# A kernel of four transformer layers: work of the first feed-forward made within the first attention's tiles

## The chip, the core and the metric

The kernel runs on one core of a Trainium2 chip. Its engines work from queues of their own: TensorE (PE) for matmuls and transposes, VectorE (DVE), ScalarE (ACT), GpSimd (POOL) and SyncE (SP), which here only starts DMAs. Engines wait for one another through semaphores. The metric is the time of the whole program on the device, in microseconds.

## The reference

x has 8 samples of 256 positions and 256 channels, the context 77 positions a sample. The part that matters is the first layer:

```python
x = x + _L0_xattn_ref(ctx_1024, _layernorm(x), mask, ...)   # 16 heads of 16
x = x + _L0_ffn_ref(_layernorm(x), w1, conv_w, conv_b, w2)

def act_quant(x):
    scale = 127.0 / clip(max(abs(x), axis=-1), 1e-05)
    return clip(round(x * scale), -128, 127) / scale
def weight_quant(w):
    scale = 1.0 / clip(mean(abs(w)), 1e-05)
    return clip(round(w * scale), -1, 1) / scale
def bit_linear(x, w): return einsum('bsd,hd->bsh', act_quant(x), weight_quant(w))
h = bit_linear(x, w1)                  # 256 -> 1024
h = silu(depthwise_conv1d(h, conv_w, conv_b))    # 3 taps
return bit_linear(h, w2)               # 1024 -> 256
```

Three further layers follow (an attention with normed heads and a mixture of experts, an attention with a position bias and a routed spline, a feed-forward with the context as weights and a ternary linear layer). The change leaves them alone, but for the centring of two weights of the second attention.

## The kernel before

The program is written engine by engine. Each engine runs through the same stages, att0 (first attention), ffn0 (first feed-forward), att1 and eight more; behind each, stage_end makes the four computing engines wait for one another. Within a stage the order of an engine's work is written out by hand, and every instruction waits in that order.

**att0** works on 16 tiles of 128 positions (u = 0 to 15, two a sample). TensorE makes the scores of tile u+2 (L775) into four banks of PSUM; VectorE adds the mask (L402) and takes the largest of each head (L404); GpSimd subtracts it (L554); ScalarE takes the exponentials (L636); TensorE transposes them (L785), multiplies by the values (L802), VectorE divides by the sums (normed: L411, L412), TensorE transposes that (turned: L809) and projects it (L815), VectorE adds it to X (residual: L419). In its pass u of the loop TensorE does: transposes of tile u, turned(u-1), scores(u+2), the value products of tile u with projected(u-1) between, and then in most passes the transposes (L738, even u) or the query product (L757, odd u) of a sample to come. VectorE does: normed(u-1), scores(u+2), residual(u-1), at u = 5 centered(), and then the statistics of a sample to come (even u: L364 to L369) or its normalisation z (odd u: L377), until u = 9. GpSimd does: the subtraction of tile u+2, and in even passes the bias added to X (L541) and a reciprocal square root (L545).

centered() subtracts from two weights of the second attention their mean over each head (a sum L426, a factor L427 and a subtraction L428 each) and makes four small scales (L429 to L432).

**ffn0** begins behind stage_end with what nothing else covers. VectorE: the statistics of samples 0 and 1 (L912 to L917); the sums of absolute values of w1 and w2 (L988); TensorE adds these over the partitions (L1099); VectorE makes the means and scales (L991 to L993), the ternary w1 in three passes (L900 to L902), two memsets of the edges of f_G, the first quantised sample (quantized(0): L924 to L936), and then the three passes over w2. GpSimd clears the value blocks of the second attention (L520) and makes 8 diagonal taps of the convolution (L1042). TensorE then transposes the quantised sample (L1108, L1110), ScalarE copies that out, TensorE makes the hidden products in four pairs (L1121), VectorE scales each (hidden: L943), and the convolution is 48 matmuls a sample (L1131).

f_w1 and f_w2, the weights as loaded, have lain at the head of the buffer "big" since about 30 us. The quantised ones, f_G and the taps lie in the part of big that the attention's tiles use; the first sample's z, its statistics and the like lie in the buffer scr, which the tiles use too.

Of the kernel before, what the change touches and what calls it, by code (L numbers as in the profile page):

```python
# [113 lines left out]
def program(nc, pack0, pack1, pack2, x_in, ctx_in, ctxT_in, w1T_in, w2T_in, ew1_in, ew2_in, out):  # L114
    with ExitStack() as ctx:
# [240 lines left out]
        def att_dve(v, ch, lay):  # L356
# [24 lines left out]
            def scores(u):  # L381
# [15 lines left out]
                else:  # L397
                    add = a_mask[:, t, :].unsqueeze(1).unsqueeze(1).broadcast_to([P, 4, C, 2 * S2])
# [22 lines left out]
            def centered():  # L421

                v.wait_ge(in_ffn, 48)
                for name, wsum in zip(("wk1", "wq1"), a_wsum):
# [61 lines left out]
            for u in range(NT + 1):  # L486
# [11 lines left out]
                if lay == 0 and u == 5:  # L498
                    centered()
# [30 lines left out]
        def att_pool(g, lay):  # L530
# [43 lines left out]
            for u in range(NT):  # L574
# [127 lines left out]
        def att_pe(pe, lay):  # L702
# [58 lines left out]
            def scores(u):  # L761
# [105 lines left out]
        f_w1q = cut(C * FF, dt=BF16).rearrange("p (c n) -> p c n", c=C)  # L867
        f_w2q = cut(FC * D, dt=BF16).rearrange("p (c n) -> p c n", c=FC)
        f_G = cut(FC * (S + 2)).rearrange("p (f s) -> p f s", f=FC)
        f_taps = cut(FC * 3 * P).rearrange("p (f j n) -> p f j n", f=FC, j=3)  # L870
        cut = Cut(scr)
        f_y = [cut(FC * S).rearrange("p (f s) -> p f s", f=FC) for _ in range(2)]
        f_aq = cut(FC * S, dt=BF16).rearrange("p (f s) -> p f s", f=FC)
        f_z = cut(T * D).rearrange("p (t d) -> p t d", t=T)
        f_zq = cut(T * D, dt=BF16).rearrange("p (t d) -> p t d", t=T)
        f_zT = cut(C * S, dt=BF16).rearrange("p (c s) -> p c s", c=C)
        f_wide1 = cut(T * P).rearrange("p (t n) -> p t n", t=T)
# [5 lines left out]
        f_stats = [cut(T * 6).rearrange("p (t s) -> p t s", t=T) for _ in range(2)]  # L883
        f_mv = [cut(T * 2).rearrange("p (t s) -> p t s", t=T) for _ in range(2)]
        f_ve = [cut(T) for _ in range(2)]
        f_rstd = [cut(T) for _ in range(2)]
# [11 lines left out]
        def ternary(ch, v, src, dst, inv):  # L898

            ch.link(v.tensor_scalar(src, src, inv, ROUND, ALU.mult, ALU.add))  # L900
            ch.link(v.tensor_scalar(src, src, ROUND, 1.0, ALU.subtract, ALU.min))
            ch.link(v.tensor_scalar(dst, src, -1.0, None, ALU.max))  # L902
# [3 lines left out]
        def ffn0_dve(v, ch):  # L906
            s = ffn0

            def stats_of(i):
                b = i % 2  # L910
                for t in range(T):
                    ch.inc(v.bn_stats(f_stats[b][:, t, :], X[:, T * i + t, :]))  # L912
                ch.sync()
                for t in range(T):
                    ch.inc(v.bn_aggr(f_mv[b][:, t, :], f_stats[b][:, t, :]))
                ch.sync()
                v.tensor_scalar(f_ve[b], f_mv[b][:, :, 1], EPS, None, ALU.add).then_inc(var_ready, 1)  # L917

            def quantized(i):

                b = i % 2
                v.wait_ge(rstd_ready, i + 1)
                for t in range(T):
                    ch.inc(v.tensor_scalar(f_z[:, t, :], X[:, T * i + t, :], f_mv[b][:, t, 0:1], f_rstd[b][:, t:t + 1],  # L924
                                           ALU.subtract, ALU.mult))
                ch.sync()
                ch.link(v.tensor_reduce(f_am, f_z[:, :, :], AX.X, ALU.max, apply_absolute_value=True))
                ch.link(v.tensor_scalar(f_am, f_am, 1e-5, None, ALU.max))
                ch.inc(v.tensor_scalar(f_deq, f_am, f_mean127[:, 0:1], None, ALU.mult))
                ch.link(v.reciprocal(f_sc, f_am))  # L930
                ch.link(v.tensor_scalar(f_sc, f_sc, 127.0, None, ALU.mult))
                v.tensor_copy(f_wide1, f_deq.unsqueeze(2).broadcast_to([P, T, P])).then_inc(s["wide1_ready"], 1)
                for t in range(T):
                    ch.inc(v.tensor_scalar(f_z[:, t, :], f_z[:, t, :], f_sc[:, t:t + 1], ROUND, ALU.mult, ALU.add))
                ch.sync()
                v.tensor_scalar(f_zq, f_z[:, :, :], ROUND, None, ALU.subtract).then_inc(z_ready, T)  # L936
# [46 lines left out]

            stats_of(0)
            stats_of(1)
            v.wait_ge(in_ffn, 48)
            for n, (f_w, wq) in enumerate(((f_w1, f_w1q), (f_w2, f_w2q))):
                v.tensor_reduce(f_tot[:, n:n + 1], f_w, AX.X, ALU.add,  # L988
                                apply_absolute_value=True).then_inc(s["wsum_ready"], 1)
            v.wait_ge(s["wsum_psum"], 1)  # L990
            ch.link(v.tensor_scalar(f_mean, bank(0, 2), 1.0 / (FF * D), 1e-5, ALU.mult, ALU.max))  # L991
            ch.inc(v.tensor_scalar(f_mean127, f_mean, 1.0 / 127.0, None, ALU.mult))
            ch.link(v.reciprocal(f_inv, f_mean))  # L993
            ternary(ch, v, f_w1, f_w1q.rearrange("p c n -> p (c n)"), f_inv[:, 0:1])
            ch.inc(v.memset(f_G[:, :, 0:1], 0.0))
            v.memset(f_G[:, :, S + 1:S + 2], 0.0).then_inc(s["w_ready"], 1)
            quantized(0)
            ternary(ch, v, f_w2, f_w2q.rearrange("p c n -> p (c n)"), f_inv[:, 1:2])
            v.sem_inc(s["w_ready"], 1)
            hidden(0)  # L1000
            for i in range(B):
                if i + 1 < B:
                    quantized(i + 1)
                if i:
                    scales(i - 1)
                if i + 2 < B:
                    stats_of(i + 2)
# [12 lines left out]

        def ffn0_pool(g):
            s = ffn0

            def rstd_of(i):
                g.wait_ge(var_ready, i + 1)
                g.tensor_tensor(f_rstd[i % 2], f_ve[i % 2], neghalf[:, 0:T], ALU.pow).then_inc(rstd_ready, 1)
# [9 lines left out]
            rstd_of(0)  # L1036
            rstd_of(1)
            vb_zeroed(g, 1)
            g.wait_ge(in_ffn, 48)
            taps = w["conv_w"].rearrange("p (f j) -> p f j", j=3)  # L1040
            for f in range(FC):
                g.tensor_tensor(f_taps[:, f, :, :], ident.unsqueeze(1).broadcast_to([P, 3, P]),  # L1042
                                taps[:, f, :].unsqueeze(2).broadcast_to([P, 3, P]), ALU.mult).then_inc(s["taps_ready"], 1)
            for i in range(B):
                if i:
                    scaled(i - 1)
                if i + 2 < B:
                    rstd_of(i + 2)
# [47 lines left out]
        def ffn0_pe(pe):  # L1096
            s = ffn0
            pe.wait_ge(s["wsum_ready"], 2)
# [1721 lines left out]
```

## Time and profile before

| | us |
|---|---|
| median of 3 runs | 1440.86 (1433.71 to 1441.57) |
| the profiled execution | 1436.02, its span 1434.2 |
| PE busy / DVE / ACT / POOL, of the span | 1131.8 / 843.7 / 381.1 / 470.4 |
| mean granted clock of TensorE | 0.857 of full |
| first attention's tiles | about 33 to 160 |
| start of the first feed-forward until its convolution | about 160 to 184 |

The page of the profile has, for each engine, the busy time and the idle time with its releaser. A chain is read from the timeline: a start, a duration, and in brackets how long the engine had been idle and whose end released it. A large sum of busy time says nothing of one stage; the windows view gives it for a stretch.

### The profile page before, as it was taken

To read this page: it belongs to the slowest core of one execution; us is meant where nothing else is said; L and a number is where in the kernel's file an instruction comes from. 1 tells how busy PE (TensorE), PEld (TensorE's weight loads), DVE (VectorE), ACT (ScalarE), POOL (GpSimd) and SP (SyncE) were. 2 spreads that over 40 slices of the span, in tenths; PEclk is the share of its full clock that TensorE was granted. 3 is DMA by queue.
4 is the path that set the end of the run, shared out by engine and by line. 5 is a ranking of instruction groups with operands and counts; after the bars stand their busy time and mean duration, and the time that the engine had idled before them with its cause. 6 is when DMAs were issued, how large, how long until landed. Compare 5 with 4: busy or idle time off the path is not lost.

```text
span 1434.2 us, 20425 instructions
## 1 busy us (share of the span) xinstructions
PE 1131.8 (79%) x7256; PEld 947.5 (66%) x7256; DVE 843.7 (59%) x1935; ACT 381.1 (27%) x798; POOL 470.4 (33%) x340
## 2 busy tenths in 40 slices
PE   6889488885688968999849999999828997915765
PEld 4778376664477845888739999999727786603433
DVE  3776678765476645888722222222575776097895
ACT  2445132221355511111112222222303443201111
POOL 3533412244556211568571100040423332002220
PEclk9799799998699989899969999999956997556575
DMA  7999000000000020000154321121200000000000
GB/s 288 392 387 363 1 0 1 19 1 0 1 1 1 2 83 1 1 1 30 55 224 152 131 84 71 37 82 46 66 24 0 1 1 1 0 0 1 15 23 22
DMA packets 43731, 93.57 MB, mean 65 GB/s; under 512 B 3821, under 2 KB 17806, under 8 KB 40838
## 3 DMA queue, kind: packets, MB, share of 16 engines
q1 hardware_dynamic: 35254, 62.24, 12.0%
q0 software_dynamic: 7104, 29.14, 5.6%
q10 hardware_dynamic: 1296, 1.18, 0.2%
q8 instruction: 47, 0.77, 0.2%
q14 instruction: 30, 0.25, 0.1%
HBM read 39.02 MB, written 51.51 MB: 63 GB/s over the span
## 4 chain that ended last, share of the span: by engine, by line
PE 65%; DVE 20%; issue 5%; ACT 4%; POOL 3%; DMA 1%; POOLq 0%; DVEq 0%; SPq 0%; ACTq 0%
PE PS L1857 9%; PE PS L1867 9%; PE PS L802 7%; PE PS L1740 3%; PE PS L1131 3%; PE PS L815 3%; PE PS L785 3%; PE PS L1394 3%; PE PS L775 3%; PE PS L757 2%; PE PS L1729 2%; PE PS L2567 2%; PE PS L684 2%; PE PS L754 1%; PE PS L1766 1%
## 5 line engine op out<-in xcount | busy, mean ns | idle before, releaser
L1857 PEld LDWEIGHTS PS<-scr 128*128 128x128 f32 x992 | 118.1, 194 | 5.1 <-issue 1.8
L1857 PE MATMUL PS<-scr 128*128 128x128 f32 x992 | 120.1, 279 | 1.5 <-ACT scr L1885 1.4
L554 POOL TENSOR_TENSOR scr<-scr,big 128x1232 f32<-128x1232 f32 x32 | 72.0, 2249 | 147.8 <-DVE big L404 147.8
L1867 PE MATMUL PS<-scr 128*128 128x256 f32 x496 | 112.2, 379 | 0.0
L1890 ACT ACTIVATE scr<-PS,W 128x128 f32<-128x128 f32 x148 | 53.5, 367 | 192.6 <-PE PS L1857 192.6
L1920 DVE TENSOR_SCALAR scr<-PS,W 128x128 f32<-128x128 f32 x148 | 51.3, 350 | 85.4 <-PE PS L1857 85.4
L641 ACT ACTIVATE big<-PS 128x512 f32<-128x512 f32 x144 | 74.6, 525 | 96.4 <-PE PS L785 96.3
L1867 PEld LDWEIGHTS PS<-scr 128*128 128x128 f32 x496 | 91.8, 190 | 11.2
L785 PE MATMUL PS<-W,scr 128*128 128x128 f32 x480 | 82.3, 294 | 21.1 <-ACT scr L636 8.1
L802 PEld LDWEIGHTS PS<-scr,big 128*128 128x128 f32 x640 | 85.2, 200 | 7.2 <-issue 5.5
L1926 DVE TENSOR_TENSOR scr<-PS,W 128x256 f32<-128x256 f32 x37 | 15.7, 425 | 124.9 <-PE PS L1867 124.9
L802 PE MATMUL PS<-scr,big 128*128 128x34 f32 (+1 forms) x640 | 87.4, 279 | 0.0
L1131 PE MATMUL PS<-big 128*128 128x256 f32 x384 | 85.5, 379 | 0.0
L785 PEld LDWEIGHTS PS<-W,scr 128*128 128x128 f32 x480 | 60.7, 158 | 32.5 <-issue 8.8
L1131 PEld LDWEIGHTS PS<-big 128*128 128x128 f32 x384 | 71.7, 190 | 9.6
L1033 POOL TENSOR_TENSOR scr<-scr 128x1024 f32<-128x1024 f32 x16 | 37.3, 2352 | 106.2 <-ACT scr L1061 106.2
L1964 POOL DMA_DIRECT2D expert_out<-scr x28 | 15.2, 544 | 163.5 <-DVE scr L1926 161.1
L1740 PE MATMUL PS<-W,scr 128*128 128x128 f32 x512 | 64.8, 288 | 2.0 <-DVE scr L1499 2.0
L1740 PEld LDWEIGHTS PS<-W,scr 128*128 128x128 f32 x512 | 62.6, 203 | 2.8 <-issue 2.7
L636 ACT ACTIVATE scr<-scr 128x1232 f32<-128x1232 f32 x48 | 58.7, 1223 | 13.7 <-POOL scr L554 12.2
L549 POOL TENSOR_TENSOR big<-big,neghalf 128x32 f32<-128x32 f32 x8 | 43.5, 5434 | 47.4 <-DVE big L437 47.4
L815 PE MATMUL PS<-W,big 128*128 128x256 f32 x192 | 54.5, 407 | 1.4 <-ACT big L646 1.4
(393 smaller groups left out, 2448.7 us busy)
## 6 DMA issues: line engine op xcount, KB each, us to landing
expert_in<-zeros SPq DMA_DIRECT2D x1, 19712.0 KB, 60.5
expert_out<-zeros SPq DMA_DIRECT2D x1, 19712.0 KB, 111.8
scr<-ew_in POOLq DMA_DIRECT2D x12, 1024.0 KB, 6.3
scr<-expert_in SPq DMA_DIRECT2D x38, 128.0 KB, 2.0
big<-ew_in POOLq DMA_DIRECT2D x4, 1024.0 KB, 8.3
expert_out<-scr POOLq DMA_DIRECT2D x28, 128.0 KB, 2.0
W<-pack SPq DMA_DIRECT2D x1, 2458.0 KB, 10.0
W<-pack SPq DMA_DIRECT2D x1, 2152.0 KB, 8.6
```

Of the source, the lines that this page charges most:

```text
L554: g.tensor_tensor(sc3, sc3, a_mx[u % 3].unsqueeze(2).broadcast_to([P, H, S2]), ALU.subtract).then_inc(s["sub_ready"], 1)
L636: a.activation(a_sc[lay][u % 3], a_sc[lay][u % 3], ACT.Exp, scale=scale).then_inc(s["p_ready"], 1)
L641: a.activation(a_PT[u % 2][:, 4 * g:4 * g + n, :], bank(ring_bank(lay, "p", u, g), n * P).rearrange("p (c n) -> p c n", c=n), ACT.Copy).th ...
L785: ins = pe.transpose(bank(b, P, k * P), a_sc[lay][u % 3][:, at:at + P], ident)
L802: ins = pe.matmul(bank(6 + u % 2, n * (DH + 1), FIRST[c] * (DH + 1)), a_PT[u % 2][:, c, :], a_VB[lay][:, c, 0:n, u // T, :], start=(c == 0 ...
L815: ins = pe.matmul(bank(6 + u % 2, D, D), a_OT[:, c, :], wo[:, c, :], start=(c == 0), stop=(c == C - 1))
L1131: ins = pe.matmul(bank(2 + p % 2, S, (f % 2) * S), f_taps[:, f, j, :], f_G[:, f, j:j + S], start=(j == 0), stop=(j == 2))
L1740: ins = pe.matmul(bank(4, P, c * P), vp[:, t, c * P:(c + 1) * P], ident, start=(t == 0), stop=(t == B - 1))
L1857: ins = pe.matmul(bank(1 + f % 4, G), e_w1[slot][:, k, f * P:(f + 1) * P], e_xT[:, k, :], start=(k == 0), stop=(k == C - 1))
L1867: ins = pe.matmul(bank(5 + t, D), e_h[:, f, t * P:(t + 1) * P], e_w2[slot][:, f, :], start=(f == 0), stop=(f == FC - 1))
L1890: a.activation(e_h[:, f, :], bank(1 + f % 4, G), ACT.Relu, bias=moe_bias(e, f)).then_inc(s["h_act"], 1)
L1920: v.tensor_scalar(e_h[:, f, :], bank(1 + f % 4, G), moe_bias(e, f), 0.0, ALU.add, ALU.max).then_inc(s["h_dve"], 1)
```

## The change

The work that prepares the first feed-forward moves into the passes of att0. VectorE, between residual(u-1) and the statistics or z of its pass: at u = 1 and 2 the sums of w1 and w2; before the scores of tile 6 (pass 4) the means, and behind residual in that pass the scales; at u = 5 to 10 one pass over a weight each; at u = 11 to 13 centered(), now in three parts, which leaves u = 5; at u = 14 and 15 the statistics of samples 0 and 1, and at u = 15 quantized(0). TensorE's cross-partition sum comes before the scores of tile 6, into two unused columns of bank 0. GpSimd makes two taps each at u = 11 to 14, and the two reciprocal square roots behind its loop. ffn0 keeps the two memsets and begins with the transposes. So that all this can lie there, f_w1q gets memory of its own, f_w2q and the taps take the place of the weights as loaded, and z and its statistics move to a free part of big. The core of the diff:

```diff
@@ att_dve, scores(u) @@
+                    if lay == 0 and u == MEANS_AT:
+                        weight_means_dve(v, ch)
@@ att_dve, the loop, behind residual(u - 1) @@
-                if lay == 0 and u == 5:
-                    centered()
+                if lay == 0:
+                    if u in (1, 2):
+                        weights_dve(v, ch, u - 1)
+                    if u == MEANS_AT - 2:
+                        weight_scales_dve(v, ch)
+                    if 5 <= u <= 10:
+                        weights_dve(v, ch, u - 3)
+                    if 11 <= u <= 13:
+                        centered(u - 11)
+                    if u in (14, 15):
+                        v.wait_ge(s["y_done"], PTILE(0, 2 * (u - 14) + T))
+                        ternary_stats(v, ch, u - 14)
+                    if u == 15:
+                        quantized(v, ch, 0)
@@ att_pool, the loop @@
+                if lay == 0 and 11 <= u <= 14:
+                    taps_pool(g, 2 * (u - 11))
+                    taps_pool(g, 2 * (u - 11) + 1)
...
+            if lay == 0:
+                ternary_rstd(g, 0)
+                ternary_rstd(g, 1)
@@ att_pe, scores(u) @@
+                if lay == 0 and u == MEANS_AT:
+                    pe.wait_ge(ffn0["wsum_ready"], 2)
+                    pe.matmul(bank(0, 2, 510), ones, f_tot, start=True, stop=True).then_inc(ffn0["wsum_psum"], 1)
@@ new @@
+        def weights_dve(v, ch, part):
+
+            s = ffn0
+            if part < 2:
+                if part == 0:
+                    v.wait_ge(in_ffn, 48)
+                v.tensor_reduce(f_tot[:, part:part + 1], (f_w1, f_w2)[part], AX.X, ALU.add,
+                                apply_absolute_value=True).then_inc(s["wsum_ready"], 1)
+                return
+            n, step = divmod(part - 2, 3)
+            src, inv = (f_w1, f_w2)[n], f_inv[:, n:n + 1]
+            if step == 0:
+                ch.link(v.tensor_scalar(src, src, inv, ROUND, ALU.mult, ALU.add))
+            elif step == 1:
+                ch.link(v.tensor_scalar(src, src, ROUND, 1.0, ALU.subtract, ALU.min))
+            else:
+                ch.link(v.tensor_scalar((f_w1q, f_w2q)[n].rearrange("p c n -> p (c n)"), src, -1.0, None, ALU.max))
+                v.sem_inc(s["w_ready"], 1)
+        MEANS_AT = 6
@@ ffn0_dve @@
-            stats_of(0)
-            stats_of(1)
-            v.wait_ge(in_ffn, 48)
...
-            v.wait_ge(s["wsum_psum"], 1)
...
-            ternary(ch, v, f_w1, f_w1q.rearrange("p c n -> p (c n)"), f_inv[:, 0:1])
             ch.inc(v.memset(f_G[:, :, 0:1], 0.0))
             v.memset(f_G[:, :, S + 1:S + 2], 0.0).then_inc(s["w_ready"], 1)
-            quantized(0)
-            ternary(ch, v, f_w2, f_w2q.rearrange("p c n -> p (c n)"), f_inv[:, 1:2])
-            v.sem_inc(s["w_ready"], 1)
             hidden(0)
@@ ffn0_pool @@
-            rstd_of(0)
-            rstd_of(1)
             vb_zeroed(g, 1)
-            g.wait_ge(in_ffn, 48)
...
-            for f in range(FC):
...
@@ ffn0_pe @@
-            pe.wait_ge(s["w_ready"], 1)
             normed(0)
             for p in range(PAIRS):
                 hidden(0, p)
             pe.wait_ge(s["taps_ready"], FC)
+            pe.wait_ge(s["w_ready"], 3)
```

## Rows read from the trace of the kernel before

**Rows 1.** Windows: stretch, length, busy us of PE PEld DVE ACT POOL, PEclk, DMA.
```profile
33.00:160.00 127.00, 110.18 (x888) 95.94 (x888) 85.02 (x128) 55.31 (x98) 49.14 (x29) 0.91 0.88 332
...
160.00:182.00 22.00, 3.44 (x16) 2.27 (x16) 20.34 (x35) 2.15 (x3) 14.18 (x11) 0.51 0.00 0
```

**Rows 2.** Timeline, 160 to 185 us: start, duration, engine, line, what; source view of L1042.
```profile
162.19 4.47 DVE L988 TENSOR_REDUCE small<-big 128x1 f32<-128x2048 f32 x2
...
163.00 3.51 POOL L520 MEMSET scr<- 128x4080 f32 x1
...
168.21 1.74 DVE L900 TENSOR_SCALAR big<-big,small 128x2048 f32<-128x2048 f32 x1
...
177.91 1.28 DVE L900 TENSOR_SCALAR big<-big,small 128x2048 f32<-128x2048 f32 x1
...
178.09 0.45 PE L1108 MATMUL PS<-W,scr 128*128 128x128 f32 x1 [10.73 <-DVE scr L936]
...
180.20 1.89 PE L1121 MATMUL PS<-scr,big 128*128 128x256 bf16 x8 [1.02 <-ACT scr L1068]
...
181.94 1.29 DVE L943 TENSOR_TENSOR big<-PS,scr 128x512 f32<-128x512 f32 x2 [0.23 <-DVE big L902]
...
184.37 10.55 PE L1131 MATMUL PS<-big 128*128 128x256 f32 x48
...
L1042 POOL TENSOR_TENSOR big<-W x8: 835/870/1819, 166.5 to 175.0; 128x384 f32<-128x384 f32 x8
```

**Rows 3.** VectorE's timeline: first statistics, and one quantisation alone.
```profile
159.91 0.75 DVE L912 BATCH_NORM_STATS2 scr<-X 128x6 f32<-128x256 f32 x2
...
185.20 0.73 DVE L924 TENSOR_SCALAR scr<-X,scr 128x256 f32<-128x256 f32 x2
...
188.34 0.43 DVE L936 TENSOR_SCALAR scr<-scr 128x512 bf16<-128x512 f32 x1
```
**Rows 4.** Timeline, end of an odd turn (1).
```profile
55.00 2.25 POOL L554 TENSOR_TENSOR scr<-scr,big 128x1232 f32<-128x1232 f32 x1 [4.56 <-DVE big L404]
...
55.40 2.32 DVE L377 TENSOR_SCALAR scr<-X,big 128x256 f32<-128x256 f32 x2
...
58.54 0.38 PE L809 MATMUL PS<-W,big 128*128 128x128 f32 x2
```

**Rows 5.** Timeline, end of an even turn (2).
```profile
62.72 2.25 POOL L554 TENSOR_TENSOR scr<-scr,big 128x1232 f32<-128x1232 f32 x1 [5.47 <-DVE big L404]
...
64.19 0.80 DVE L369 TENSOR_SCALAR big<-big 128x2 f32<-128x2 f32 x1
...
64.92 1.26 POOL L541 TENSOR_TENSOR X<-X,W 128x512 f32<-128x512 f32 x1
...
65.67 0.44 PE L809 MATMUL PS<-W,big 128*128 128x128 f32 x2 [0.81 <-DVE big L412]
```

**Rows 6.** Timeline, end of turn 5, with centered().
```profile
85.93 1.17 DVE L427 TENSOR_SCALAR small<-small 128x32 f32<-128x32 f32 x1
...
87.13 0.69 DVE L428 TENSOR_TENSOR W<-W,small 128x512 f32<-128x512 f32 x1
...
91.07 0.44 PE L809 MATMUL PS<-W,big 128*128 128x128 f32 x2 [2.54 <-DVE big L412]
```

**Rows 7.** Windows, 92 to 93 us; TensorE's timeline at the next turn.
```profile
92.00:93.00 1.00, 1.00 (x12) 0.84 (x7) 0.69 (x1) 0.00 (x0) 0.00 (x0) 0.62 1.03 387
...
100.56 0.38 PE L809 MATMUL PS<-W,big 128*128 128x128 f32 x2
```

**Rows 8.** Timelines of GpSimd and TensorE, ends of turns 10 and 12.
```profile
127.37 2.25 POOL L554 TENSOR_TENSOR scr<-scr,big 128x1232 f32<-128x1232 f32 x1 [5.48 <-DVE big L404]
...
129.35 0.38 PE L809 MATMUL PS<-W,big 128*128 128x128 f32 x2
...
141.26 2.25 POOL L554 TENSOR_TENSOR scr<-scr,big 128x1232 f32<-128x1232 f32 x1 [5.49 <-DVE big L404]
...
142.43 0.44 PE L809 MATMUL PS<-W,big 128*128 128x128 f32 x2
```

More of the change, by code:

```diff
@@ L419, in residual, with centered @@
                 v.tensor_tensor(X[:, u, :], bank(6 + u % 2, D, D), X[:, u, :], ALU.add).then_inc(s["y_done"], 1)
-            def centered():
-                v.wait_ge(in_ffn, 48)
-                for name, wsum in zip(("wk1", "wq1"), a_wsum):
+            def centered(part):
+                if part < 2:
+                    name, wsum = ("wk1", "wq1")[part], a_wsum[part]
                     w3 = w[name].rearrange("p (g d) -> p g d", d=DH)
@@ L882, in program @@
         f_amax = cut(S)
[L883 to L886, printed above, removed]
         f_am = csmall(T)
@@ L896, in program, with ternary_stats @@
                     "wide2_ready", "row2_psum", "row2_ready", "scaled_ready", "aq_ready", "o_psum", "o_kept")
[L898 to L902, printed above, removed]
+        def ternary_stats(v, ch, i):
+            b = i % 2
+            for t in range(T):
+                ch.inc(v.bn_stats(f_stats[b][:, t, :], X[:, T * i + t, :]))
+            ch.sync()
+            for t in range(T):
+                ch.inc(v.bn_aggr(f_mv[b][:, t, :], f_stats[b][:, t, :]))
+            ch.sync()
+            v.tensor_scalar(f_ve[b], f_mv[b][:, :, 1], EPS, None, ALU.add).then_inc(var_ready, 1)
@@ new lines, in quantized @@
+        def quantized(v, ch, i):
+            b = i % 2
+            v.wait_ge(rstd_ready, i + 1)
+            for t in range(T):
+                ch.inc(v.tensor_scalar(f_z[:, t, :], X[:, T * i + t, :], f_mv[b][:, t, 0:1], f_rstd[b][:, t:t + 1],
+                                       ALU.subtract, ALU.mult))
+            ch.sync()
+            ch.link(v.tensor_reduce(f_am, f_z[:, :, :], AX.X, ALU.max, apply_absolute_value=True))
+            ch.link(v.tensor_scalar(f_am, f_am, 1e-5, None, ALU.max))
+            ch.inc(v.tensor_scalar(f_deq, f_am, f_mean127[:, 0:1], None, ALU.mult))
+            ch.link(v.reciprocal(f_sc, f_am))
+            ch.link(v.tensor_scalar(f_sc, f_sc, 127.0, None, ALU.mult))
+            v.tensor_copy(f_wide1, f_deq.unsqueeze(2).broadcast_to([P, T, P])).then_inc(ffn0["wide1_ready"], 1)
+            for t in range(T):
+                ch.inc(v.tensor_scalar(f_z[:, t, :], f_z[:, t, :], f_sc[:, t:t + 1], ROUND, ALU.mult, ALU.add))
+            ch.sync()
+            v.tensor_scalar(f_zq, f_z[:, :, :], ROUND, None, ALU.subtract).then_inc(z_ready, T)
@@ new lines, in weight_means_dve, with weight_scales_dve, taps_pool @@
+        def weight_means_dve(v, ch):
+            v.wait_ge(ffn0["wsum_psum"], 1)
+            ch.link(v.tensor_scalar(f_mean, bank(0, 2, 510), 1.0 / (FF * D), 1e-5, ALU.mult, ALU.max))
+        def weight_scales_dve(v, ch):
+            ch.inc(v.tensor_scalar(f_mean127, f_mean, 1.0 / 127.0, None, ALU.mult))
+            ch.link(v.reciprocal(f_inv, f_mean))
+        def taps_pool(g, f):
+            if f == 0:
+                g.wait_ge(ffn0["w_ready"], 2)
+            taps = w["conv_w"].rearrange("p (f j) -> p f j", j=3)
+            g.tensor_tensor(f_taps[:, f, :, :], ident.unsqueeze(1).broadcast_to([P, 3, P]),
+                            taps[:, f, :].unsqueeze(2).broadcast_to([P, 3, P]), ALU.mult).then_inc(ffn0["taps_ready"], 1)
@@ L907, in ffn0_dve @@
             s = ffn0
[L909 to L936, printed above, removed]
             def hidden(i):
@@ L1002, in ffn0_dve @@
                 if i + 1 < B:
-                    quantized(i + 1)
+                    quantized(v, ch, i + 1)
                 if i:
@@ L1097, in ffn0_pe @@
             s = ffn0
-            pe.wait_ge(s["wsum_ready"], 2)
-            pe.matmul(bank(0, 2), ones, f_tot, start=True, stop=True).then_inc(s["wsum_psum"], 1)
             def normed(i):
```

40 lines of the change are left out of this document (18 added, 22 removed).

## The prediction, made before the changed kernel was run

> **What bounds the kernel now.** I read the trace in the order in which the change meets it. First the busy time by stretch [rows 1]: in the first attention's tiles (33 to 160 us) TensorE is busy 110 of 127 us, VectorE 85; in the 22 us behind them TensorE is busy 3.4 us and VectorE 20.3 us. So there are two regimes, and the change takes work out of the second and puts it into the first.
>
> Then the handover [rows 2]. VectorE's first instruction of the feed-forward is at 159.91 [rows 3]. From there two sums of absolute values (2.28 us each), one cross-partition sum on TensorE, the means, three passes over w1 and the first quantisation run one behind the other, until TensorE gets its first transposes at 178.09; the convolution begins at 184.37. Nothing on TensorE covers this: 24.5 us from 159.91 to 184.37 is a pure chain.
>
> Then one tile of the attention, as a chain of turns. I call turn u what the engines do in pass u of the loops, and mark its start by TensorE's transposes L809 (turned(u-1)). VectorE's order in a turn is normed(u-1), scores(u+2), residual(u-1), the extras that the change adds to, statistics (even u) or z (odd u), and next normed(u), for which L809 of the next turn waits. The reader is to see two things in [rows 4, 5]. GpSimd starts L554 (2.25 us) just before VectorE's residual and is still in it when the extras begin. And a tensor_scalar of VectorE that meets it doesn't end before L554 does: in the odd turn two L377 take 2.32 us and end 0.47 behind L554's end (57.72 against 57.25), where such a pair alone takes 0.73 (L924, [rows 3]); in the even turn L369, two elements a partition, takes 0.80 and ends at 64.99, L554 at 64.97. In the turn with centered(), L427 ends at 87.10 in the same way after 1.17 us for 32 elements [rows 6]. So the free time that VectorE seems to have in a tile lies mostly elsewhere (it waits for the scores), and where the extras stand there is none: in odd turns L809 comes 3.54 us behind L554's start with z done 0.8 us before it, in even turns it comes 2.95 behind it, set by VectorE.
>
> **The change, part by part.**
>
> *Removed behind the tiles.* After the stage's end TensorE can transpose at once, since weights and z exist. What is left is the piece from 178.09 to 184.37, 6.3 us, less about 0.75: the first half of the eight L1121 was done near 181.15, L943 came at 181.94, behind the second weight's passes [rows 2]: 5.5 us. At full clock this piece would be about 1 us shorter; GpSimd's memset L520 of 3.5 us, which now starts together with this piece, may hold VectorE's two small memsets and so L943 by up to 1.3 us. So 24.5 - 5.5 = **19.0 us gained** (17.7 to 20.1). The second weight's passes ran beside other work and give no more. From the convolution on nothing differs.
>
> *Added to the tiles.* A weight pass takes 1.28 us with GpSimd idle and 1.74 us beside the taps [rows 2]; started behind a wait for L554 I take 1.2, since the start is then already paid (L377 above). The statistics of one sample took 1.15 (two of them from 159.91 to 162.19, [rows 2, 3]); as L369's end is late I count 1.2. From L554's start to L809 it gives: odd turns 2.25 + 1.2 + 0.73 (z) + 0.68 (normed and hand-over, the 64.99 to 65.67 of [rows 5]) = 4.86 against 3.54, **+1.32**; even turns 2.25 + 1.2 + 1.2 (statistics, which no longer run under L554) + 0.68 = 5.33 against 2.95, **+2.38**. Turn by turn:
> - Turns 1 and 2 have the sums of 2.28 us, which ran at this length beside GpSimd's memset and first tap [rows 2]. The extras begin 0.4 behind L554's start (55.40, [rows 4]). Turn 1: 0.4 + 2.28 + 0.73 + 0.68 = 4.1 against 3.54: +0.6. Turn 2: 0.4 + 2.28 + 1.2 + 0.68 = 4.6 against 2.95: +1.6.
> - Turn 4: the cross-partition sum on TensorE before the scores (two small matmuls, 0.3 to 0.6 us, 0.4 taken), the mean behind it fits into VectorE's wait for the scores; the scales are tensor_scalar and reciprocal, 0.4 us behind L554, with the statistics behind them: 4.53 against 2.95. Together +2.0.
> - Turn 5: centered() leaves (TensorE waited 2.54 us for it [rows 6]), a pass comes: 1.32 - 2.54 = -1.2. Turn 6: 7.13 + 2.38 = 9.5 us, against 9.5 before (91.07 to 100.56), when the clock was low [rows 7]: 0.
> - Turns 7 and 9 +1.3 each, turn 8 +2.4. Turn 10, without statistics: 4.13 against the 1.98 from 127.37 to 129.35 (L554, L809) [rows 8]: +2.15.
> - Turns 11 and 12: centered() in two parts. Each is a sum (beside L554), L427 (waits for L554) and L428 (0.69, [rows 6]). From L554's start 2.25 + 0.2 + 0.69 + 0.68 = 3.8, against 3.54 in turn 11, an odd one, and 1.17 in turn 12 [rows 8]: +0.3 and +2.6. L428 reads two tensors of SBUF, and behind L554 GpSimd now goes on with a tap (median 0.87 us, [rows 2]) or with L541 (1.26, [rows 5]). No row shows such an instruction of VectorE beside one of GpSimd; held, it costs 0.75 and 1.3 more. I take half: +0.6 and +3.3.
> - Turn 13: four tiny tensor_scalars behind L554, 3.1 against 1.2 as in turn 12, a tap may come between: +2.2. Turn 14: the first statistics, 1.2 us, ahead of normed(14): +1.2.
> - Turn 15: second statistics 1.2 and the first quantisation, 3.57 us from 185.20 to 188.77 [rows 3], both ahead of normed(15), which until now follows residual(14) with nothing between and has TensorE waiting for it. So all of it is on the path: 4.8, with the rstd on GpSimd between up to 5.3: +5.0.
>
> The sum is 0.6 + 1.6 + 2.0 - 1.2 + 0 + 1.3 + 2.4 + 1.3 + 2.15 + 0.6 + 3.3 + 2.2 + 1.2 + 5.0 = **22.5 us lost** (20 to 26). The rule of the Trainium skill that bears on it is in "SBUF — State Buffer", section "SBUF: two separate sides": the port pair that VectorE shares with GpSimd is an exclusive lock, kept for the whole instruction, for VectorE's two-port modes and for two SBUF inputs against a GpSimd instruction that reads SBUF. For the tensor_scalars the trace agrees (2.32 us for 0.73). For L428 no row here shows it; by the page turns 11 and 12 cost the whole 2.05 us, and the sum would be 23.5 instead of 22.5.
>
> The eight taps cost GpSimd 0.87 us each; in turns 11 to 13 it waits before L554 for 2 us or more ([rows 8] have 5.5 before those of turns 10 and 12), so two a turn fit, and their wait for the weights is met a turn earlier. Behind that wait would stand the next L554, due later. Nothing of SP's or of GpSimd's DMA queue moves. The new place of the buffers costs nothing.
>
> *The clock.* The wait of 2.54 us of turn 5 had a price of its own: the granted clock went from full (2.4 GHz) to half (1.2 GHz) at about 92.4, and the turn took 9.5 instead of 7.1 us [rows 7]: 2.4 us. In a plain even turn TensorE waits 0.81 us [rows 5]. Now it waits 2.5 us or more in turns 2, 4, 6, 8, 12, 13 and 15 and 2.1 in turn 10. Where a fall comes on an odd turn, the turn is bound by TensorE: 7.8 + 3.3 = 11.1, against 9.1, so about 2 us each (3 in turn 3). I can't tell how many of these waits drop the clock; none costs 0, nearly all cost 12. I take three, **6 us lost**.
>
> Net: 22.5 + 6 - 19.0 = **+9.5 us**. The profiled execution had 1436.0 us (span 1434.2, and 1.8 around it); the median of the runs is 1440.9, so it was one of the quicker. From one I get 1445.5, from the other 1450.4; I forecast **1448 us**.
>
> **The rivals.**
> 1. *The clock falls in nearly every second turn.* For it: the new waits are as long as the one that did it or longer. Against it: one fall is all that the trace has inside these tiles after their start, and one case says nothing of how often a wait of this length does it. Price 12 instead of 6: 1454. In the Trainium skill, "TensorE: Matmul & The Clock Gate", section "HAM oscillation — how this bites in real kernels", a loop that waits once in each pass goes back to half clock every pass; by it this rival would be the forecast. The trace has one such wait, and it agrees.
> 2. *Faster: VectorE's passes run beside L554.* If the large passes get through (they did get their turns between the taps, 1.74 us against 1.28), a pass costs 1.25 us right behind residual: odd turns hide it, even ones cost 0.7, turns 12, 13, 14 and 15 cost 1.7, 0.5, 1.2 and 4.8, turns 5 and 6 give back 2.7 and 1.7. Some 7.5 us lost against 19 won: -11.5, 1427. It decides at the point where the tiles grow by less than 19 us. Against it: every tensor_scalar that met L554 ended behind it.
> 3. *A draw.* The lock holds but costs less than I add up (15 to 18 us, few falls of the clock): -3 to +4, about 1438.
>
> **How the numbers follow.** Forecast 0.50 (its own range 1441 to 1455), rival 1 0.17, rival 2 0.12, rival 3 0.21. The range 1432 to 1461 leaves out rival 2 and the far end of rival 1. About 0.5% (7 us) is what a measurement can tell from no change. Slower by more: all of rival 1 and four fifths of the forecast, 0.57. Within: the rest of the forecast and nearly all of rival 3, 0.30. Faster: rival 2 and a little, 0.13.
>
> **What would show it.** In the changed kernel the weight passes (1.2 us of work) must read 2.5 to 3 us in the tiles and end about 1.2 behind L554; turn 8 must take 9.5, turn 15 9.7 us; the last residual comes 23 to 32 us later, the convolution begins 5.5 us behind the stage's end. I am wrong if passes of 1.25 us stand beside a running L554, if TensorE's waits before L809 stay under 1 us in turns 6 to 10, or if the stage after begins later than 7 us behind the tiles.

## The result, and the profile after

The changed kernel is slower: 1459.22 us (median of 4 runs, 1448.65 to 1463.21) against 1438.96 beside it, a ratio of 1.0153 with a 95% interval of 1.0113 to 1.0193. That is 20 us; the forecast was 1448, or 9.5 us more than before. The time lies in the stated range (1432 to 1461) and on the forecast side, but only 2 us under the top of that range and above the forecast's own (1441 to 1455): the loss is about twice what was summed.

The profiled execution of the changed kernel had 1463.2 us (span 1461.5), at the upper end of its runs. Its lines have other numbers: L554 is now L569, L541 is L556, L809 is L833, L815 is L839, L1121 is L1156, L1131 is L1166.

Windows view of the changed kernel, columns as in [rows 1]:

```profile
33.00:202.00 169.00, 134.10 (x885) 115.36 (x885) 103.02 (x158) 55.52 (x97) 60.39 (x39) 0.76 0.66 250
202.00:211.50 9.50, 7.36 (x28) 4.29 (x29) 2.46 (x6) 2.54 (x4) 3.50 (x1) 0.50 0.00 0
```

The stretch of the tiles has grown by over 40 us and the one behind it has shrunk from 22 to under 10. And there is one number that was 0.91 before: the granted clock of the tiles is 0.76 of full.

The handover, TensorE's timeline of the changed kernel (start, duration):

```profile
203.13 2.07 PE L839 MATMUL PS<-W,big 128*128 128x256 f32 x4 [0.47 <-ACT big L667]
205.84 0.47 PE L1143 MATMUL PS<-W,big 128*128 128x128 f32 x1 [0.64 <-DVEq L185]
...
211.55 11.69 PE L1166 MATMUL PS<-big 128*128 128x256 f32 x48
```

The transposes follow the last projection by 0.6 us, and the convolution begins 5.7 us behind their start. That is the piece of the old chain that is left, and it is as long as forecast (5.5 us). But the convolution begins at 211.55, where it began at 184.37 [rows 2]: 27.2 us later, the whole difference of the two spans (27.3). Behind it these two executions take 1249.8 and 1250.0 us. In the later experiments, on four chips, this rest took 1241 to 1262 us, within about 4 us of one another on one chip; so each kernel is compared only with runs of the kernel before beside it on its own chip.

An even turn (6), timelines of VectorE, GpSimd and TensorE of the changed kernel; compare [rows 5]:

```profile
107.29 2.25 POOL L569 TENSOR_TENSOR scr<-scr,big 128x1232 f32<-128x1232 f32 x1 [8.81 <-DVE big L406]
...
107.71 2.92 DVE L967 TENSOR_SCALAR big<-big 128x2048 f32<-128x2048 f32 x1
...
109.50 2.25 POOL L556 TENSOR_TENSOR X<-X,W 128x512 f32<-128x512 f32 x1
...
112.58 0.69 PE L833 MATMUL PS<-W,big 128*128 128x128 f32 x2 [3.15 <-DVE big L414]
```

The pass over the weights starts 0.4 us behind L569's start, takes 2.92 instead of 1.28 us and ends at 110.63, 1.1 behind L569's end (109.54). It then held off L556 in its turn, which took 2.25 instead of 1.26. TensorE waited 3.15 us. Now the clock, windows view at both ends of the fall that follows:

```profile
111.00:112.00 1.00, 0.00 (x0) 0.00 (x0) 0.93 (x6) 0.00 (x0) 0.77 (x2) 0.74 1.02 385
112.00:113.00 1.00, 0.42 (x2) 0.29 (x2) 0.49 (x2) 0.00 (x0) 0.68 (x1) 0.50 1.04 391
...
121.00:122.00 1.00, 1.00 (x4) 0.86 (x4) 1.00 (x1) 0.00 (x0) 0.00 (x0) 0.64 1.03 387
```

It is at half (1.2 GHz) from 111.5 to 121.7 us, nearly the whole of turn 7. In that turn VectorE's pass costs nothing:

```profile
117.67 2.25 POOL L569 TENSOR_TENSOR scr<-scr,big 128x1232 f32<-128x1232 f32 x1 [4.99 <-DVE big L406]
...
120.80 1.22 DVE L969 TENSOR_SCALAR f_w1q<-big 128x2048 bf16<-128x2048 f32 x1
...
124.67 0.38 PE L833 MATMUL PS<-W,big 128*128 128x128 f32 x2
```

TensorE is so late with L839 that the residual and the pass come after L569, the pass runs at its own 1.22 us, and TensorE doesn't wait at L833. This turn is bound by TensorE at half clock: 12.1 us.

All turns in us, from the starts of L809 or its successor. The forecast column has the 22.5 us of the port and the queue, without the 6 us of the clock. The last column is an experiment that is told below:

| turn | before | forecast | changed kernel (TensorE's wait at its end) | waits filled |
|---|---|---|---|---|
| 1 | 8.1 | 8.7 | 12.7 (0) | 12.7 |
| 2 | 7.1 | 8.7 | 8.7 (2.4) | 8.7 |
| 3 | 7.8 | 7.8 | 12.6 (0) | 7.8 |
| 4 | 7.1 | 9.1 | 8.8 (2.4) | 8.8 |
| 5 | 10.5 | 9.3 | 11.1 (0) | 9.0 |
| 6 | 9.5 | 9.5 | 9.5 (3.2) | 9.5 |
| 7 | 7.7 | 9.1 | 12.1 (0) | 12.0 |
| 8 | 7.1 | 9.5 | 9.5 (3.2) | 9.5 |
| 9 | 7.8 | 9.1 | 12.5 (0) | 9.0 |
| 10 | 6.2 | 8.3 | 8.5 (2.2) | 8.6 |
| 11 | 7.7 | 8.3 | 12.7 (0) | 8.5 |
| 12 | 5.3 | 8.6 | 8.9 (3.5) | 8.9 |
| 13 | 5.4 | 7.6 | 10.5 (0.4) | 8.1 |
| 14 | 4.7 | 5.9 | 5.6 (1.1) | 6.9 |
| 15 | 4.7 | 9.7 | 9.1 (5.5) | 9.1 |
| sum | 106.7 | 129.2 | 152.7 | 137.1 |

The even turns are as forecast to 0.3 us. The odd ones from 3 to 13 are 2 to 5 us longer than forecast. The clock fell behind each even turn up to 12 and behind turn 15, seven times. What I had taken as three falls at 2 us was six falls inside the tiles at some 3 us, one at their end, and one in turn 1, which the kernel before didn't have in its profiled execution.

The profiled executions are single draws: 46 us more in the tiles, 17.6 less behind them and a start 1.2 earlier give 27 us, where the medians differ by 20. An execution of 1448.65 us was among the runs of the changed kernel, with a granted clock of 0.858 over the whole where the profiled one had 0.848; its trace isn't there.

### The profile page after: what moved, and what is told of

It reads as the page before. It is cut to its first block, busy times and chain, and to the rows that moved or that the text cites. A ratio compares the mean times of both kernels' runs of the same rounds, so it can differ in the third digit from the quotient of the medians.

```text
span 1461.5 us, 20426 instructions
## 1 busy us (share of the span) xinstructions
PE 1157.0 (79%) x7256; PEld 966.9 (66%) x7256; DVE 842.2 (58%) x1935; ACT 381.3 (26%) x798; POOL 471.4 (32%) x340
## 4 chain that ended last, share of the span: by engine, by line
PE 65%; DVE 20%; issue 5%; ACT 4%; POOL 4%; DMA 1%; POOLq 0%; SPq 0%; DVEq 0%; ACTq 0%
PE PS L1890 9%; PE PS L1900 9%; PE PS L826 7%; PE PS L839 3%; PE PS L1166 3%; PE PS L1773 3%; PE PS L1427 3%; PE PS L778 3%; PE PS L809 3%; PE PS L799 3%; PE PS L1762 2%; PE PS L2600 2%; PE PS L705 1%; PE PS L833 1%; PE PS L775 1%
## 5 line engine op out<-in xcount | busy, mean ns | idle before, releaser
L569 POOL TENSOR_TENSOR scr<-scr,big 128x1232 f32<-128x1232 f32 x32 | 71.9, 2248 | 175.8 <-DVE big L406 175.8
L826 PEld LDWEIGHTS PS<-scr,big 128*128 128x128 f32 x640 | 95.1, 220 | 8.4 <-issue 5.9
L809 PE MATMUL PS<-W,scr 128*128 128x128 f32 x480 | 83.7, 297 | 20.9 <-ACT scr L657 8.1
L826 PE MATMUL PS<-scr,big 128*128 128x34 f32 (+1 forms) x640 | 96.3, 297 | 0.0
L1166 PE MATMUL PS<-big 128*128 128x256 f32 x384 | 86.6, 382 | 0.0
L809 PEld LDWEIGHTS PS<-W,scr 128*128 128x128 f32 x480 | 62.0, 161 | 32.8 <-issue 9.2
L1166 PEld LDWEIGHTS PS<-big 128*128 128x128 f32 x384 | 72.5, 192 | 9.9
L839 PE MATMUL PS<-W,big 128*128 128x256 f32 x192 | 61.1, 447 | 1.4 <-ACT big L667 1.4
L657 ACT ACTIVATE scr<-scr 128x1232 f32<-128x1232 f32 x48 | 58.7, 1223 | 13.5 <-POOL scr L569 12.0
```

The costliest lines, as they stand in the source:

```text
L569: g.tensor_tensor(sc3, sc3, a_mx[u % 3].unsqueeze(2).broadcast_to([P, H, S2]), ALU.subtract).then_inc(s["sub_ready"], 1)
L657: a.activation(a_sc[lay][u % 3], a_sc[lay][u % 3], ACT.Exp, scale=scale).then_inc(s["p_ready"], 1)
L809: ins = pe.transpose(bank(b, P, k * P), a_sc[lay][u % 3][:, at:at + P], ident)
L826: ins = pe.matmul(bank(6 + u % 2, n * (DH + 1), FIRST[c] * (DH + 1)), a_PT[u % 2][:, c, :], a_VB[lay][:, c, 0:n, u // T, :], start=(c == 0 ...
L839: ins = pe.matmul(bank(6 + u % 2, D, D), a_OT[:, c, :], wo[:, c, :], start=(c == 0), stop=(c == C - 1))
L1166: ins = pe.matmul(bank(2 + p % 2, S, (f % 2) * S), f_taps[:, f, j, :], f_G[:, f, j:j + S], start=(j == 0), stop=(j == 2))
```

## The experiments

**Port, queue or clock.** Three kernels put one more instruction of VectorE into the kernel before, in turns 6, 8 and 10, where the change puts its passes. One is a pass of tensor_scalar, one a sum of about the same length (an estimate from L404, 1.44 us for 1232 elements), one a sum of 2.28 us. A tensor_reduce didn't wait for GpSimd in the trace of before: L426 took 0.68 us both beside L554 and behind it. In these kernels L554 is L557, L541 is L544 and L809 is L812.

```diff
@@ kernel before, att_dve, behind residual(u - 1) @@
+                if lay == 0 and u in (6, 8, 10):
+                    v.wait_ge(in_ffn, 48)
+                    ch.link(v.tensor_scalar(f_w1, f_w1, 1.0, None, ALU.mult))
+                    ch.link(v.tensor_reduce(spare, f_w1[:, 0:1152], AX.X, ALU.add))
+                    ch.link(v.tensor_reduce(spare, f_w1[:, 0:2048], AX.X, ALU.add))
```

Each kernel has one of the last three lines: b_scalar_even the pass, b_reduce_same the sum over 1152 elements, b_reduce_long the one over 2048. The pass multiplies f_w1 by one in place, the sums are used by nothing.

> The kernel before, with one pass of tensor_scalar over w1 (128x2048, times 1.0) added behind the residual in turns 6, 8 and 10. Shared port and clock (my theory): the pass ends 1.2 us behind L554, turn 8 takes 9.5 instead of 7.2 us and turn 10 8.3 instead of 6.15, TensorE waits about 3.2 us before L809 and its clock falls behind each, so that turns 9 and 11 take about 12 instead of 7.7: in all 15 to 20 us slower. Port without clock: turns 9 and 11 stay at 7.7, 7 us slower. No port: turn 8 takes 7.9, in all 2 us slower.

> The kernel before, with a tensor_reduce of 1152 columns (about 1.3 us, as long as a pass of tensor_scalar alone) in the same three places; its result is used for nothing. My theory: it runs beside L554, so turn 8 takes 7.8 (plus 0.6), turn 10 6.5, TensorE waits 1.4 us, no fall of the clock, turns 9 and 11 stay at 7.7: 2 us slower in all. If the added work costs by its place in the queue and not by the port, it costs what the tensor_scalar costs.

> The kernel before, with a tensor_reduce of 2048 columns (2.28 us) in the same three places; its result is used for nothing. No port is held, but TensorE waits some 2.4 us before L809. If the wait alone drops the clock: turn 8 takes 8.8, turn 10 7.5 and turns 9 and 11 about 12: 4.6 us from the waits and 8 to 13 from the clock. If the clock theory is wrong: 4.6 us slower and turns 9 and 11 stay at 7.7.

Measured against the kernel before: 1.0103 (1.0048 to 1.0157), 1.0036 (1.0011 to 1.0062) and 1.0102 (1.0050 to 1.0154). The intervals overlap a little; it is the traces that tell the first two apart. Turn 8 in VectorE's and TensorE's timelines, first b_scalar_even:

```profile
119.53 2.92 DVE L502 TENSOR_SCALAR big<-big 128x2048 f32<-128x2048 f32 x1
...
124.40 0.69 PE L812 MATMUL PS<-W,big 128*128 128x128 f32 x2 [3.15 <-DVE big L412]
```

b_reduce_same:

```profile
114.46 1.34 DVE L502 TENSOR_REDUCE small<-big 128x1 f32<-128x1152 f32 x1
...
116.90 0.64 DVE L369 TENSOR_SCALAR big<-big 128x2 f32<-128x2 f32 x1
...
118.21 0.44 PE L812 MATMUL PS<-W,big 128*128 128x128 f32 x2 [2.03 <-DVE big L412]
```

b_reduce_long:

```profile
114.97 2.27 DVE L502 TENSOR_REDUCE small<-big 128x1 f32<-128x2048 f32 x1
...
119.20 0.69 PE L812 MATMUL PS<-W,big 128*128 128x128 f32 x2 [2.50 <-DVE big L412]
...
131.74 0.38 PE L812 MATMUL PS<-W,big 128*128 128x128 f32 x2
```

Two instructions of about 1.3 us that both start 0.4 us behind L557's start: the tensor_scalar takes 2.92, the tensor_reduce 1.34. Turn 8 takes 9.5 and 8.3 us, turn 10 8.3 and 6.7. So the port is real and worth 1.1 to 1.6 us a turn. My 7.8 for b_reduce_same was too low: its L369 now met the bias (L544, 116.25 to 117.51) and ended with it, 0.64 us for two elements. With that TensorE waited 2.03 us instead of the 1.4 expected, and its clock fell, which I had not expected either: 5 us slower, not 2.

The third kernel separates the clock. Its sum takes 2.27 us beside L557, as long as alone, so it doesn't meet the port, and yet after its wait of 2.50 us the next turn (9) takes 12.5 us. Turn 11, after a wait of 1.35, takes 7.8. After b_reduce_same's 2.03 turn 9 takes 11.1, after b_scalar_even's 3.15 it takes 13.5; before, it takes 7.8. Turns 9 and 11 have no added work in any of the three. They grow behind a long wait of TensorE, whether a port or a longer sum made it. In b_scalar_even two more turns grew: the fall behind turn 5 lasted 20 us, from 92.4 to 112.9, through turns 6 (10.7) and 7 (13.0).

**Filling the waits.** If that is so, the changed kernel must get its odd turns back when TensorE is kept busy with nothing, while VectorE's delays stay.

```diff
@@ changed kernel, att_pe, turned(u) @@
+                fill = {2: 8, 4: 8, 5: 4, 6: 8, 7: 4, 8: 8, 9: 4, 10: 8, 12: 8, 14: 4, 15: 20}.get(u, 0) if lay == 0 else 0
+                if fill:
+                    pe.wait_ge(s["y_done"], PTILE(lay, u))
+                    for _ in range(fill):
+                        pe.matmul(bank(6 + (u + 1) % 2, 128), ident, ident, start=True, stop=True)
                 pe.wait_ge(s["on_ready"], PTILE(lay, u) + 1)
```

This is a_filled_all. A first form, a_filled, had eight matmuls for u = 2, 4, 6, 8, 10 and 12 alone.

> The changed kernel, with eight matmuls of the identity by itself (about 1.8 us) issued by TensorE just before it waits for VectorE at the start of turns 3, 5, 7, 9, 11 and 13, into a bank that is free then; their result is used for nothing. Clock theory: the waits of 2.2 to 3.5 us shrink to 0.4 to 1.7, the clock stays at full, the odd turns 3 to 13 take 8 to 9 us instead of 11 to 12.7, the even ones stay as they are: 15 to 20 us quicker than the changed kernel. If the odd turns are long for another reason (the port, VectorE's work), nothing is won.

Measured 1.0097 (1.0076 to 1.0117): less than expected, 2 to 8 us quicker than the changed kernel by its 1.0112 and 1.0153 on other chips. Turns 3, 5, 7, 9, 11 and 13 took 7.8, 9.0, 9.2, 9.0, 8.4 and 8.9 us in the profiled execution, 52.3 in all instead of 71.5. But the clock now fell in turns 6 and 10, behind waits of 1.1 us at the end of odd turns, which had become bound by VectorE, in turn 13 behind one of 1.68, and still at the end. That is why the next form fills more. In this trace the convolution begins at 194.45, 17 us earlier than in the changed kernel; behind it this execution took 7.8 us more (1257.8).

The changed kernel itself (after_again) and the new form ran on one chip:

> The changed kernel once more, to stand beside the next two on one chip and to show how much the tiles differ from execution to execution. Theory: each wait of TensorE of 2 us or more is followed by a fall of the clock; the even turns take the same time to 0.1 us as in the first execution (8.7, 8.8, 9.5, 9.5, 8.5, 8.9), the odd ones differ with the moment of the fall.

> The changed kernel, with matmuls of no use ahead of every longer wait of TensorE in the tiles: eight in turns 3, 5, 7, 9, 11 and 13, four in turns 6, 8, 10 and 15, twenty in turn 16. If the long turns are the port plus the clock, as I say: the clock stays at full in the tiles, what is left is the port's part that the prediction summed, 22.5 us over the kernel before (turns 1 to 16 about 129 us, against 107), and it is 12 to 20 us quicker than the changed kernel on the same chip. If the clock isn't the cause, the turns stay as long as in the changed kernel.

On one chip: the changed kernel 1453.43 us, 1.0112 (1.0060 to 1.0164) of before; with its waits filled 1436.78 us, 1.0016 (0.9984 to 1.0048). The two intervals don't meet. So 14 us (by the ratios) to 17 us (by the medians) of the changed kernel's time are the clock's, and with the clock up it is as quick as the kernel before: the port's part and the handover's gain cancel. Two lines of windows of a_filled_all, first the tiles (from 49 to 202 us the changed kernel has 0.77), then the fall of turn 1 that is left in them:

```profile
49.00:187.00 138.00, 123.06 (x980) 109.07 (x980) 98.90 (x144) 50.58 (x90) 52.37 (x35) 0.93 0.69 262
51.00:60.00 9.00, 9.00 (x33) 8.03 (x33) 6.05 (x8) 1.50 (x2) 2.25 (x1) 0.50 1.05 410
```

The last column of the table has its turns. Against my expectation the clock didn't stay at full: falls are left in turn 1, in turn 7, behind a wait of 1.36 us, and in turn 14, from 172.7 to 176.2 us, behind one of 2.62 us at the end of turn 13, which had no fill. With 8.4 us for turn 1 (from a_filled), 9.0 for turn 7 (as turns 5 and 9) and 5.6 for turn 14 (as in the changed kernel, at full clock) its tiles would take 128.5, 22 us over before; 22.5 were forecast for the port and the queue.

after_again also shows how steady the pattern is: its sum of turns is 152.7 us again, and no turn differs by more than 0.1, the odd ones included, which I had expected to differ.

**The place.** The same six passes, put ahead of the scores:

```diff
@@ changed kernel, att_dve @@
+                if lay == 0 and 5 <= u <= 10:
+                    weights_dve(v, ch, u - 3)
                 if u + 2 < NT:
                     scores(u + 2)
...
-                    if 5 <= u <= 10:
-                        weights_dve(v, ch, u - 3)
```

> The changed kernel with the six weight passes of turns 5 to 10 put ahead of the scores, where VectorE waits for TensorE, instead of behind the residual. My theory: in even turns GpSimd is idle there and the pass costs nothing (turns 6 and 8 take 7.2, turn 10 6.2, no fall of the clock behind them), in odd turns it meets L556 and costs up to 1.3: turns 5 to 10 take about 47 us instead of 63, the whole is 14 to 18 us quicker than the changed kernel. If the amount of work decides and not its place: no gain.

Measured 1.0050 (1.0025 to 1.0075) against before. From turn 5 to the end of turn 10 it takes 49.4 us, the changed kernel 63.1. Turns 6, 8 and 10 take 7.2, 7.2 and 6.2 us, with no fall behind them. The 49.4 us still hold the fall behind turn 4, which makes turn 5 12.5 us. The changed kernel didn't run on this chip; by its ratios on two others (1.0153 and 1.0112) the new place is worth 9 to 15 us, where 14 to 18 were expected.

**The last turns.** The statistics and the quantisation, which the change puts behind the residual of turns 14 and 15, ahead of the scores of their turn (there are none in these turns) and so of the residual:

```diff
@@ changed kernel, att_dve @@
+                if lay == 0:
+                    if u in (14, 15):
+                        v.wait_ge(s["y_done"], PTILE(0, 2 * (u - 14) + T))
+                        ternary_stats(v, ch, u - 14)
+                    if u == 15:
+                        quantized(v, ch, 0)
                 if u + 2 < NT:
                     scores(u + 2)
```

The same lines behind the residual are gone.

> The changed kernel, with the first statistics and the first quantisation in turns 14 and 15 put ahead of the residual, where VectorE waits 3.4 us for TensorE, instead of behind it. My theory: turn 14 goes from 5.6 to 4.7, turn 15 from 9.1 to about 5.7 (statistics and quantisation are 4.8 us and the gap is 3.6), TensorE no longer waits 5.5 us, and the convolution begins 4 to 6 us earlier. If the place doesn't matter: no gain.

Measured 1.0118 (1.0082 to 1.0154), not to be told from the changed kernel by its time. The trace shows turns 14 and 15 with 4.5 and 5.6 us instead of 5.6 and 9.1, as expected, and a wait of 1.75 instead of 5.47 us at their end; this is 4.7 us of 1460. The clock ahead of it differed too: this trace has no fall in turns 1 and 11.

**Everything in the gaps.** The last two findings together:

```diff
@@ changed kernel, att_dve, between normed(u - 1) and scores(u + 2) @@
+                if lay == 0:
+                    for part in {0: (0,), 1: (1,), 4: (2,), 6: (3,), 8: (4,), 10: (5,), 12: (6, 7)}.get(u, ()):
+                        weights_dve(v, ch, part)
+                    if u in (11, 12):
+                        v.wait_ge(s["y_done"], PTILE(0, 2 * (u - 11) + T))
+                        ternary_stats(v, ch, u - 11)
+                    if u == 14:
+                        for part in range(3):
+                            centered(part)
+                    if u == 15:
+                        quantized(v, ch, 0)
```

In place of the block behind the residual. MEANS_AT is 4 with the scales right behind the means, and GpSimd makes four taps in pass 11 and two each in 12 and 14, the reciprocal roots in 12.

> All the moved work, each piece put where VectorE waits for TensorE and GpSimd is mostly idle: the sums ahead of the scores in turns 0 and 1, the passes ahead of the scores in turns 4, 6, 8, 10 and (two) 12, statistics in 11 and 12, centering in 14, quantisation in 15, both ahead of the residual. My theory: no turn grows by more than 1 us, no wait of TensorE is above 1.2 us, the clock stays at full from the first turns on, the tiles take about as long as before (110 us or less from turn 1 to the last), and the 19 us of the handover remain: 15 to 22 us quicker than the kernel before, 1.0 to 1.5%. If moved work always costs in the tiles what it saves behind them: no change against the kernel before.

Measured 1427.28 us, 0.9858 (0.9836 to 0.9879) of before: 20 us quicker than before. Turn 6 of it, VectorE:

```profile
92.47 1.22 DVE L965 TENSOR_SCALAR big<-big 128x2048 f32<-128x2048 f32 x1
94.00 1.44 DVE L405 TENSOR_TENSOR scr<-PS,big 128x1232 f32<-128x1232 f32 x1 [0.32 <-DVE big L965]
```

The pass stands in the gap of 1.3 to 1.5 us in which VectorE used to wait for the scores, GpSimd is idle, and the turn takes 7.2 us. The tiles take 109.7 us. Longer than before are turn 2 (7.7, the means), 12 (6.6), 14 (6.5) and 15 (5.4), in all 4.5 us, and turn 3: its clock fell, behind a wait of 1.27 us, and it took 11.1. So turns 3, 12 and 14 grew by more than the 1 us expected, and three waits (1.27, 1.23 and 1.80 us) were above 1.2. On the other side the fall of turn 6 is gone, since centered() has left turn 5. The convolution begins at 170.10, 14.3 us earlier than in the trace of before, which was taken with the first result and not beside this one; what makes up the other 6 us of the 20 no trace here shows.

Then it ran once more, unchanged (gaps_again), beside a kernel that also fills the waits that are left in it (gaps_warm):

```diff
@@ gaps, att_pe, turned(u) @@
+                fill = {2: 4, 12: 4, 14: 7, 15: 3}.get(u, 0) if lay == 0 else 0
+                if fill:
+                    pe.wait_ge(s["y_done"], PTILE(lay, u))
+                    for _ in range(fill):
+                        pe.matmul(bank(6 + (u + 1) % 2, 128), ident, ident, start=True, stop=True)
@@ gaps, ffn0_pe @@
+            for _ in range(6):
+                pe.matmul(bank(7, 128), ident, ident, start=True, stop=True)
```

> The kernel with all moved work in VectorE's gaps once more, beside the next one on the same chip: 1.2 to 1.6% quicker than the kernel before, as in its first run.

> The kernel with all moved work in VectorE's gaps, and matmuls of no use on TensorE ahead of its waits in turns 3 (four), 13 (four), 15 (seven) and 16 (three) and, six, behind the first transposes of the feed-forward. Clock theory: no fall in turn 3 (minus 3.3 us) and a full clock at the handover (from the last L831 to the convolution 7 us instead of 9.6): 3 to 6 us quicker than without them, 1.6 to 1.9% quicker than the kernel before. If the clock plays no part there: no gain.

The first measured 0.9877 (0.9826 to 0.9928), the second 0.9846 (0.9816 to 0.9876). In the trace of the second turn 3 took 7.8 us and the clock stayed at full from turn 2 through the handover. But turn 1 took 12.7 us at half clock in this execution. And gaps_again had no fall at the handover without any filling: its wait of 1.79 us at the end of turn 14 wasn't followed by one, where the 1.80 us of the first run were. From the last L831 to the convolution it took 6.9 us, the first run 9.6. So the convolution began at 167.11 us in gaps_warm and at 167.03 in gaps_again. The intervals overlap widely: a gain of the filling beyond the placing isn't shown.

## Why the prediction was right, and which term was too small

The way, slower, was right and rested on the right mechanisms. That the time also fell into the range is partly luck: two of the four runs (1461.7 and 1463.2) lie above it.

*The port.* "A tensor_scalar of VectorE that meets it doesn't end before L554 does" held for each pass in a full-clock turn, and the price followed: +2.38 forecast for an even turn, 7.1 to 9.5 measured in turn 8. Summed over the tiles 22.5 were forecast, and some 22 is what a_filled_all gives with the clock up. For L428 (now L430) half of the wait was taken, 1.0 us of 2.05; the trace of turn 12 decides it:

```profile
173.16 1.17 DVE L429 TENSOR_SCALAR small<-small 128x32 f32<-128x32 f32 x1
174.36 1.70 DVE L430 TENSOR_TENSOR W<-W,small 128x512 f32<-128x512 f32 x1
...
176.73 0.69 PE L833 MATMUL PS<-W,big 128*128 128x128 f32 x2 [3.46 <-DVE big L414]
```

L430 took 1.70 us instead of 0.69: L556 ran until 175.50. The Trainium skill, "SBUF — State Buffer", section "SBUF: two separate sides", has this case too (two SBUF inputs against a GpSimd instruction that reads SBUF), and it was right. In turn 11 of the changed kernel nothing was held: at half clock the residual came after L569. At full clock it was: in a_filled_all L430 of turn 11 met a tap and took 1.26.

*The gain.* 19.0 us were forecast. With the clock up, from the last L809 to the convolution it is 27.2 us before and 6.9 in a_filled_all: 20.3. As the changed kernel ran, at half clock, 9.6: 17.6. The clock took 2.7 us of the gain, and 1.1 more of the first convolution (11.69 against 10.55 us). With the clock up 22 us lost and 20.3 won leave 1.5, and a_filled_all's 1.0016 is 2 us.

*The signs.* The passes of 2.92 us, turn 8 with 9.5 and the convolution 5.7 us behind the start of its stage came as forecast. Turn 15 took 9.1 us instead of 9.7. The last residual came 46 us later (205.31 against 159.33) and not 23 to 32; by the table the surplus is the clock's.

*The clock.* This is the term that was mis-sized. "I take three, **6 us lost**": the measured share is 14 to 17 us by a_filled_all, which doesn't get all of it back, and 24 in the tiles of the one profiled execution (152.7 less 128.5), of which some 4 are turn 1's. Two things were wrong. How often: I gave the case that nearly every wait drops the clock a chance of 0.17, with the argument that one case says little. Over the 13 profiled executions of all kernels here TensorE waited 34 times for 2.0 us or more at L809; at 33 of them the granted clock went to half, in the wait or within 3 us behind it, the exception a wait of 2.19 (a_quant_ahead, turn 10). The waits of 0.8 to 0.9 us of plain even turns never were followed by a fall; between 1.1 and 1.8 some were and some not. And how much: I took 7.8 + 3.3 = 11.1 us for an odd turn with a fall. In the tiles of the changed kernel half clock lasts 7 to 10 us at a time, and an odd turn takes up to 12.7. Rival 1 had the mechanism right, and even its 12 us were too few. The Trainium skill, "TensorE: Matmul & The Clock Gate", section "HAM oscillation — how this bites in real kernels", tells of a loop that waits for a DMA in each pass and goes back to half clock in each. The trace agrees with that pattern, every second turn here, though the waits are for VectorE and last 2.2 to 3.5 us in turns 2 to 12. Two smaller slips: the fall in the kernel before was at 92.2 rather than 92.4 us, and the wait of 2.5 us or more forecast for turn 13 was 0.4, since that turn ran at half clock; with the clock up (a_filled_all) it was 2.6.

*The rivals.* Rival 2, passes beside a running L554, is out: 2.92 us against 1.34 for a sum of the same length. Rival 3, a draw, has the number that a_filled_all measures, 1.0016, but not its reason: the port and the queue cost 22 us there and not 15 to 18, and the handover gave 20.3.

*What stays open.* Turn 1 took 8 to 9 us in nine executions and 12.7 at half clock in four (after, after_again, a_filled_all, gaps_warm). In those four the granted clock had come back to full at 43 us already, TensorE was early, waited 1.7 us at the start of turn 1, and the clock fell again. In the nine it was at half until 50 us or later, and there was no such wait. It isn't the change that decides this: gaps and gaps_again drew the one, gaps_warm, the same up to there, the other. What does wasn't tried, nor was its share in the spread of the runs. So some 3 us of the 27 between the two profiled executions (turn 1 longer by 4.6, its start earlier by 1.2) can't be put down to the moved work.

## What to carry to other kernels

Work moved beside a busy stage was free here only in the gap where its engine really waited, and only where it didn't meet an instruction of GpSimd that held the port: look at the timeline of one turn, not at the busy share. A wait that this made on TensorE cost twice, its own length and, in 33 of the 34 cases of 2.0 us or more, a stretch at half clock, of 7 to 10 us in the tiles of the changed kernel and of 3.5 to 20 in the other kernels. The same work, put where VectorE waited for TensorE with GpSimd mostly idle, turned 1.1 to 1.5% slower into 1.2 to 1.4% quicker.

## What the runs showed of the hardware that was not expected

- When L569 of turn 6 ended, both VectorE's pass and GpSimd's L556 were due; the pass, which had waited longer, went first and L556 took 2.25 us instead of 1.26. In turn 12 L430, which came only behind L429, 0.1 us after L556's start, lost to L556 and took 1.70 instead of 0.69. That the longer wait decides is not shown by these two cases.
- Useless matmuls are worth time: 84 of them, some 1% of the kernel (1453.4 to 1436.8 us, 1.0112 to 1.0016), with nothing else changed.
- A turn at half clock hides VectorE's additions: in turn 7 the pass cost nothing. The two losses of this change mostly don't add up in one turn; from turn 2 to 13 they alternate, the port in even turns, the clock in odd ones.
